# Self-attention of a Perceiver block: the turned x moves from the projection banks to the banks of the output sums, and its high part moves ahead of the fourth exponential

## The reference

```python
x = x + _L0_xattn_ref(_layernorm(x), ctx_1024, ctx_1024, ...)
x = x + _L0_attn_ref(_layernorm(x), wq, wk, wv, wo)
x = x + _L0_ffn_ref(_layernorm(x), W_in, b_in, W_out, b_out)

def _L0_attn_ref(x, wq, wk, wv, wo):          # 16 heads of 64, 64 tokens per batch
    q, k, v = (jnp.einsum('bsd,hed->bhse', x, w) for w in (wq, wk, wv))
    scores = jnp.einsum('bhse,bhte->bhst', q, k) / 8
    weights = jax.nn.softmax(jnp.where(causal_mask, -1e9, scores))
    heads = jnp.einsum('bhst,bhte->bhse', weights, v)
    return heads.transpose(0, 2, 1, 3).reshape(b, s, 1024) @ wo.T
```

## Time and profile before

| | |
|---|---|
| median of 3 runs | 637.76 us (636.15 to 639.42) |
| the profiled execution: its time, its span | 638.59 us, 636.8 us |
| self-attention in the span | about 303 to 555 us |
| one group of the steady part (from its X 0 to the next one's) | 31.63 us |
| TensorE's mean granted clock | 0.983 of full speed |

### The profile page before, as it was taken

One profiled execution on the slowest core, in us unless ns is written; L12 is line 12 of the kernel. 1 busy time (PEld: TensorE's weight loads), 2 busy tenths in 40 slices (PEclk: granted clock), 3 DMA queues, 4 the chain that ended last, 5 costly groups with the idle time before them and its releaser, 6 DMA issues. The chain is left out here.

```text
span 636.8 us, 17469 instructions
## 1 busy us (share of the span) xinstructions
PE 591.1 (93%) x6765; PEld 514.9 (81%) x6770; DVE 464.2 (73%) x977; ACT 377.1 (59%) x1011; POOL 190.2 (30%) x243
## 2 busy tenths in 40 slices
PE   6689999999999899997798999999999999899897
PEld 3578888898889788996687888888989898644597
DVE  4557788888878778875899756565666656678797
ACT  3567788888878788873322424343433333558884
POOL 6522233333333333672411212121212111260400
PEclk9789999999999999999899999999999999999999
DMA  6995767777768768840400000000000000000012
GB/s 205 259 245 147 196 150 192 161 204 158 209 149 205 162 166 220 209 154 1 134 2 11 3 3 1 3 1 2 3 3 1 2 3 2 2 0 2 0 50 83
DMA packets 37073, 58.93 MB, mean 93 GB/s; under 512 B 6913, under 2 KB 15233, under 8 KB 36993
## 3 DMA queue, kind: packets, MB, share of 16 engines
q1 hardware_dynamic: 29328, 42.75, 26.7%
q10 hardware_dynamic: 4592, 8.78, 4.9%
q0 software_dynamic: 3072, 6.30, 4.2%
HBM read 17.96 MB, written 2.10 MB: 31 GB/s over the span
## 5 line engine op out<-in xcount | busy, mean ns | idle before, releaser
L704 ACT ACTIVATE Pr<-pS,nmax 128x256 f32<-128x256 f32 x256 | 120.0, 483 | 27.0 <-DVE nmax L818 25.9
L818 DVE TENSOR_REDUCE nmax<-pS 128x2 f32<-128x512 f32 x128 | 87.4, 683 | 23.5 <-PE pS L542 22.2
L1045 POOL TENSOR_TENSOR a_Pr<-a_Pr,a_rinv 128x512 f32<-128x512 f32 x32 | 32.7, 1044 | 182.9 <-DVE a_rinv L1327 182.9
L552 PE MATMUL pT<-ident,Pr 128*128 128x128 f32 x512 | 78.9, 277 | 2.7 <-DVE wraw L823 2.4
L542 PE MATMUL pS<-Kst,Qst 96*128 96x256 f32 x256 | 59.1, 314 | 14.4 <-ACT Pr L704 5.5
L1213 ACT ACTIVATE a_Pr<-a_Pr 128x512 f32<-128x512 f32 x32 | 20.2, 631 | 78.9 <-DVE a_Pr L1319 78.9
L552 PEld LDWEIGHTS pT<-ident,Pr 128*128 128x128 f32 x512 | 60.4, 143 | 3.9 <-issue 3.9
L542 PEld LDWEIGHTS pS<-Kst,Qst 96*128 96x128 f32 x256 | 40.8, 196 | 22.7 <-issue 12.1
L704 ACT ACTIVATION_READ_ACCUMULATOR Pr<-pS,nmax 128x1 f32 x256 | 54.8, 214 | 0.0
L324 POOL DMA_DIRECT2D Qst<-QSh x60 | 30.3, 508 | 75.1 <-PE pS L542 71.4
L59 PE MATMUL a_pJ<-Kst,XTh 128*128 128x512 f32 x64 | 27.9, 437 | 3.0 <-ACT a_V L1208 3.0
(11 more groups left out here) (365 smaller groups left out, 2079.6 us busy)
## 6 DMA issues: line engine op xcount, KB each, us to landing
Kst<-WO_ints SPq DMA_DIRECT2D x96, 128.0 KB, 3.3
CT<-ctxT ACTq DMA_DIRECT2D x16, 512.0 KB, 5.0
Kst<-KSh SPq DMA_DIRECT2D x62, 128.0 KB, 3.1
Qst<-QSh POOLq DMA_DIRECT2D x64, 64.0 KB, 3.1
Qst<-QSh SPq DMA_DIRECT2D x64, 64.0 KB, 2.8
Kst<-KSl SPq DMA_DIRECT2D x31, 128.0 KB, 3.3
Qst<-QSl POOLq DMA_DIRECT2D x32, 64.0 KB, 2.8
Qst<-QSl SPq DMA_DIRECT2D x32, 64.0 KB, 2.7
```

The costliest lines, as they stand in the source:

```text
L552: last = pe.transpose(pT[s % 2][:, t, k, :], Pr[s % 2][:, t, P * k:P * k + P], ident[:, :])
L704: act.activation(Pr[c % 2][:, t, :], pS[c % 2][:, t, :], ACT.Exp, bias=nmax[c % 2][:, t:t + 1], accum_out=rsum[par][:, c // 4, 2 * (c % 4) ...
L818: dve.tensor_reduce(nmax[s % 2][:, :], pS[s % 2][:, :, :], AX.X, ALU.max, negate=True).then_inc(maxed, 1)
L1045: pool.tensor_tensor(rows, rows, rinv[s][:, :].unsqueeze(2).to_broadcast([P, 8, SQ]), ALU.mult).then_inc(weighted, 1)
```

## The change

X no longer goes through the two projection banks. A new function `turn_x` turns it into columns 0 to 255 of `pO` 0 and 1 and waits for the normalised x alone. It has a semaphore of its own, `x_turned`. The projection banks are handed out to 14 fillings per group in place of 16 (`EV`), with the same parity for every filling that remains. `x_high` and `x_low` read `pO`. On ScalarE the two `x_high` now stand ahead of exponential 3, on VectorE the order stays. `turn_x` stands in TensorE's queue where X stood.

```diff
-    EV = 16
+    EV = 14
...
             def bank_read(kind, part, quad):
-                if kind == "X":
-                    pe.wait_ge(xt_lo, 2 * (quad - 1) + part + 1)
-                elif kind == "Y":
+                if kind == "Y":
...
+            def turn_x(quad, part):
+                pe.wait_ge(ln_xn, 2 * quad)
+                for t in range(2):
+                    last = pe.transpose(pO[part][:, t, :], XN[:, t, P * part:P * part + P], ident[:, :])
+                last.then_inc(x_turned, 1)
...
             def fill(bank, kind, part, quad):
                 out = pJ[bank]
-                if kind == "X":
-                    pe.wait_ge(ln_xn, 2 * quad)
-                    for t in range(2):
-                        last = pe.transpose(out[:, P * t:P * t + P], XN[:, t, P * part:P * part + P], ident[:, :])
-                elif kind in "QK":
+                if kind in "QK":
...
-            def x_high(r, part, bank):
-                act.wait_ge(proj, r + 1)
-                act.activation(XT[HI][:, part, :], pJ[bank][:, 0:2 * P], ACT.Copy).then_inc(xt_hi, 1)
+            def x_high(i, part):
+                act.wait_ge(x_turned, 2 * i + part + 1)
+                act.activation(XT[HI][:, part, :], pO[part][:, 0:2, :].rearrange("p t n -> p (t n)"), ACT.Copy
+                               ).then_inc(xt_hi, 1)
...
                 fills("V", 2)
+                if not last:
+                    x_high(i, 0)
+                    x_high(i, 1)
                 exps(i, 3)
-                fills("X", 0)
-                fills("X", 1)
```

More of the change, by code:

```diff
@@ L974, in self_attention @@
         ln_st, ln_mv, ln_ve, ln_rs, ln_xn = sem("ln_st"), sem("ln_mv"), sem("ln_ve"), sem("ln_rs"), sem("ln_xn")
-        proj, xt_hi, xt_lo = sem("proj"), sem("xt_hi"), sem("xt_lo")
+        proj, x_turned, xt_hi, xt_lo = sem("proj"), sem("x_turned"), sem("xt_hi"), sem("xt_lo")
         by_act, by_dve = sem("by_act"), sem("by_dve")
@@ L1003, in plan @@
             for kind, s in LAST if last else PLAN:
-                if kind in ("score", "turn", "weigh"):
+                if kind in ("score", "turn", "weigh", "X"):
                     work.append((kind, s, None))
@@ L1175, in body @@
                         weigh(i, s)
+                    elif kind == "X":
+                        turn_x(i + 1, s)
                     else:
@@ L1236, in fills @@
                             turned_w_in(EV * i + k, part, k % 2)
-                        elif kind == "X":
-                            x_high(EV * i + k, part, k % 2)
                         else:
@@ L1299, in normalize, with x_low @@
                                       mv[:, t, 0:1], rstd[:, t:t + 1], ALU.subtract, ALU.mult).then_inc(ln_xn, 1)
-            def x_low(quad, part, bank):
-                dve.wait_ge(xt_hi, 2 * (quad - 1) + part + 1)
-                dve.tensor_tensor(XT[LO][:, part, :], pJ[bank][:, 0:2 * P], f32(XT[HI][:, part, :]), ALU.subtract
+            def x_low(i, part):
+                dve.wait_ge(xt_hi, 2 * i + part + 1)
+                dve.tensor_tensor(XT[LO][:, part, :], pO[part][:, 0:2, :].rearrange("p t n -> p (t n)"),
+                                  f32(XT[HI][:, part, :]), ALU.subtract
                                   ).then_inc(xt_lo, 1)
@@ L1392, in fills @@
                         r = EV * i + k
-                        if kind == "X":
-                            x_low(i + 1, part, k % 2)
-                        elif kind == "Y":
+                        if kind == "Y":
                             add_rows(r, i, part, k % 2)
@@ L1407, in body @@
                 fills("V", 3)
-                fills("X", 0)
-                fills("X", 1)
+                if not last:
+                    x_low(i, 0)
+                    x_low(i, 1)
                 sums(i, 2)
```

## The result

In the comparison made for the result the changed kernel took 629.25 us (median of 4 runs, 628.75 to 630.97) against 636.95 us before (4 runs, 633.87 to 639.42). The ratio is 0.989, with a 95% interval of 0.9862 to 0.9918. The profiles agree with these: 5.0 us come from the stage that was changed. One of the 35 runs of the kernel before in the first of the later comparisons took 820.59 us at a mean granted clock of 0.654, and the ratios leave it out.

What follows compares the result with a forecast made beforehand. TensorE's work plus 0.69 us of idling was taken to bound a steady group; seven groups at 0.66 us give 4.6 us, so the median 637.76 becomes 633.1 us, range 631.4 to 635.2 (main case alone 631.8 to 634.4).

Steps and rivals of the forecast that it cites:

- What bounds the kernel: Steady self-attention group: TensorE's work plus 0.69 us idle, 0.54 ahead of X 1 and 0.15 ahead of Q 0.
- The new chain from X 0 to Q 0: Turns, high parts, low parts, then Q 0 in the third group: Q 0 moves from 385.06 to 384.40, 0.66 us a group.
- an earlier X 0 would bring nothing: At X 0 behind V 2's copy: at most some 0.1 us to win, without effect because VectorE's queue sets Q 0.
- Sum: Self-attention stage: seven groups at 0.66 us each give 4.6 us less.
- What the change adds: ScalarE's exponential 3 starts 0.67 us later, still covered by 0.71 us before VectorE's sum 3; nothing added to TensorE.
- Seven groups: All seven self-attention groups, the first two included, gain the same 0.66 us.
- The clock is no rival: TensorE's clock: half speed only in the first group ahead of X, full in steady groups; the change only shortens gaps.
- The rule against the rows: VectorE's two subtractions: if each starts only at the end of the one before, 0.53 us a group, 634.1 us.
- the serial chain: VectorE's low parts without overlap, Q 0 at 384.53: 3.7 us in all; part of the smaller-gain rival, chance 0.09.
- the term for the spread of the medians: Whole kernel: the part of the range 631.8 to 634.4 left for medians of runs that lay 636.15 to 639.42.
- the outer range: Whole kernel: 631.4 to 635.2 us, taking in the main case, larger and smaller gains and a partial giving back.

Runs made afterwards that it cites:

- the first of the later comparisons: The changed kernel, with no further edit, timed again against the kernel before: 631.76 us (12 runs), ratio 0.9926.
- the two larger comparisons: The changed kernel, with no further edit, timed twice more against the kernel before: 631.76 and 631.01 us, ratios 0.9926 and 0.9919.
- the second profile of the kernel before: The kernel before, with no edit, profiled and timed again against its own other runs: 636.08 us (12 runs), ratio 0.9995.

## Why the prediction was right in its mechanism and wrong in its range

- *What bounds the kernel* was read rightly: a steady group got as much shorter as Q 0 came earlier.
- *The new chain from X 0 to Q 0.* Right in its order: X 1 directly behind X 0, the high parts waiting for the turn, the low parts behind V 3's copy, 0.15 us to Q 0. The size was 0.66 and is 0.71. The low part of part 0 was put at 0.63 us behind the start of V 3's copy, by ScalarE; it was 0.60, by VectorE's own queue. The rest, 0.02 us, is that the low parts took 0.89 us from the first start to Q 0 (378.87 - 377.98) in place of 0.91. The sentence that an earlier X 0 would bring nothing doesn't fit the prediction's own sum, which has ScalarE 0.03 us behind VectorE's queue (383.49 against 383.46). That 0.03 us was won: X 0 came 0.08 us earlier, and the high part 0.41 us behind it in place of 0.47. By the distances in the rows either would have been enough; no run separates them. Two smaller sizes were off without touching Q 0: the turns of the weights start 0.43 us behind X 0 in place of 0.54, so TensorE waits 0.34 us ahead of Q 0 and not some 0.2, and ScalarE idles 0.38 us ahead of the high parts and not 0.5.
- *Sum*: 4.6 us, measured 5.0 between the same two places of the profiles, and 4.7 and 5.2 by the medians of the two larger comparisons.
- *What the change adds*: the exponential 0.67 us later and covered by 0.71. Measured: it starts 1.20 us behind V 3's last product (378.02 - 376.82) in place of 0.68, so 0.52 us later, and is covered by 0.8 us. With ScalarE's order alone it was 1.4 us later and still cost nothing.
- *Seven groups, the first two included*: right, 5.00 us over the seven, against the first profile of the kernel before (0.71 by the first Q 0, 1.44 by the second).
- *"The clock is no rival"*: right for the steady groups (1.00). In the first group it differed between executions of one kernel. In the second profile of the kernel before it stayed at 0.50 for longer and cost 0.69 us, as much as the change gives in a group. In the changed kernel it cost nothing that shows: X 0 of the first group started 10.54 us behind the first normalisation at a clock of 1.00 and 11.96 us at one of 0.50 to 0.83, and Q 0 13.68 and 13.69.
- *The rule against the rows.* The section that the prediction names (the Trainium skill, VectorE: DVE Perf Modes, The DRAIN you can't avoid) says that the next VectorE instruction does not start until the pipe has emptied. It also says that a next one that is not held starts earlier, which the prediction left out. In this trace the two low parts run back to back within 0.74 us, 0.41 us each, so here the second starts at 378.31 while the first ends at 378.39. The overlap of the earlier rows holds here as well, and the 634.1 us of the serial chain did not come.
- *The step that failed is the term for the spread of the medians*: "the rest for medians of runs that lay 636.15 to 639.42". With the gain's own spread it allowed 1.3 us on either side of the forecast for a median (1.7 below it in the outer range, 631.4). The measured 629.25 lies 3.9 us below 633.1: 0.4 us is the mis-sized sum, and 3.5 us is the place of the medians. Of these 637.76 was high for the kernel before (636.1 to 637.0 in the comparisons since), and 629.25 low for the changed one (631.8 and 631.0 since). In the profiles the spread comes from the part ahead of self-attention, nearly all of it cross-attention, which took 300.2 to 304.2 us in three of one and the same kernel; the runs without a profile don't show where theirs lies. The three runs shown spread over 3.3 us, and the profile of the forecast had a 3 us wait for a transfer with the clock down behind it, in a stage that the prediction left out because the change does not touch it. Which executions a comparison met was chance: of the later medians of the changed kernel 631.8 lies inside 631.4 to 635.2, and 631.0 below it.

## What to carry to other kernels

When two holds lie side by side (a bank and a queue), price them together and one by one: here they were worth 0.24, 0.00 and 0.71 us. When a change is worth less than the spread of the runs, look through the whole profile for waits that may differ from run to run, and widen the range by them, even in stages that the change does not touch; then settle the size by a window between two fixed points inside the changed stage, which here repeated within 0.03 us over three profiles of either kernel. Where several products share a wait for several parts, let each wait for its own part (0.32 us a group here).

## What the runs showed that was not expected

- The wait of X 0 for V 2's copy was short and still cost time. The copy ended 0.27 us behind the start of V 3's last product both in the kernel before and in the run with the wait put back; without the wait X 0 starts at 0.24 us. With it, X 0 started at 0.32 us in the one and at 0.41 us in the other. Why the same wait took 0.09 us more in the second kernel was not separated.
- TensorE's busy time per group fell by 0.36 us with the same instructions, 0.28 because transposes that had stood in two pairs came to stand in a row and 0.08 because X 0 overlaps the product ahead of it for longer; and a group 99.97% busy still had 0.08 us to give.
- The first transfer that TensorE waits for in cross-attention came in two classes, a wait of 4.2 to 4.9 or of 7.3 to 8.5 us, for the same program. With the short wait and none for `Kst` self-attention started at 298.66 to 300.16 us (three profiles), with the long one at 301.06 to 303.95 (six); the three profiles with a wait for `Kst` had 300.18, 303.03 and 304.19.
